# An adaptive-layernorm block with attention and mixture of experts: gates in the last evictions, a three-pass output projection, the second normalisation on ScalarE

## The reference

```python
mod = (silu(c) @ wmod).reshape(B, 6, 1, -1)
sa, ca, ga, sb, cb, gb = (mod[:, i] for i in range(6))
ga = (2 * (ga >= 0) - 1) * maximum(abs(ga), 0.25)       # gb alike
h = layernorm(x) * (1 + ca) + sa
x = x + ga * attention(h, Wq, Wk, Wv, Wo)               # 2 query heads of 128, one key/value head,
                                                        # rotary angles, causal softmax
h = layernorm(x) * (1 + cb) + sb
x = x + gb * experts(h)
# experts: gate = softmax(h @ Wg + bg); thr = sigmoid(h @ Wt + bt) * 0.125
#          w = gate - thr where that is >= 0, else 0; w /= sum(w) (1 for a sum of 0)
#          out = sum over 8 experts e of w[e] * (gelu(h @ W1[e] + b1[e]) @ W2[e] + b2[e]), hidden size 1024
```

## Time and profile before

| what | us |
|---|---|
| median of 3 runs | 1739.81 (1739.69 to 1741.04) |
| the profiled execution | 1741.29 |
| its span, first to last instruction | 1739.5 |
| PE busy | 1723.0 (99%) |
| DVE busy | 1213.2 (70%) |
| POOL busy | 995.8 (57%) |
| ACT busy | 994.9 (57%) |

### The profile page before, as it was taken

One profiled execution on the slowest core, in us unless ns is written; L12 is line 12 of the kernel. 1 busy time (PEld: TensorE's weight loads), 2 busy tenths in 40 slices (PEclk: granted clock), 3 DMA queues, 4 the chain that ended last, 5 costly groups with the idle time before them and its releaser, 6 DMA issues.

```text
span 1739.5 us, 26367 instructions
## 1 busy us (share of the span) xinstructions
PE 1723.0 (99%) x8408; PEld 1448.2 (83%) x8408; DVE 1213.2 (70%) x2275; ACT 994.9 (57%) x1797; POOL 995.8 (57%) x1649
## 2 busy tenths in 40 slices
PE   8999999999999999999999999999999999999998
PEld 7889888898888888888888888888888888888887
DVE  6777778767676666666666678766666666666666
ACT  3766666655665555555555566555555555555553
POOL 5644455336264655647484849374847566574843
PEclk9999999999999999999999999999999999999999
DMA  4000000012111111111112121222301011111202
GB/s 114 26 25 19 26 25 25 11 34 69 23 52 25 50 25 49 37 37 37 37 49 30 47 33 39 61 67 80 110 25 49 25 49 37 37 37 37 37 12 61
DMA packets 92059, 72.54 MB, mean 42 GB/s; under 512 B 11025, under 2 KB 90129, under 8 KB 91921
## 3 DMA queue, kind: packets, MB, share of 16 engines
q1 hardware_dynamic: 91776, 70.79, 15.2%
q10 hardware_dynamic: 144, 0.07, 0.0%
HBM read 62.32 MB, written 8.52 MB: 41 GB/s over the span
## 4 chain that ended last, share of the span: by engine, by line
PE 83%; DVE 2%; issue 1%; ACT 1%; POOL 0%; DVEq 0%; ACTq 0%; POOLq 0%
PE bank L1088 13%; PE bank L1086 13%; PE bank L1087 13%; PE bank L1042 11%; PE bank L1044 11%; PE bank L1043 11%; PE bank L966 2%; PE bank L992 1%; PE bank L1006 1%; PE bank L954 1%; PE bank L955 1%; PE bank L953 1%; PE bank L888 1%; PE bank L878 1%; PE bank L987 1%
## 5 line engine op out<-in xcount | busy, mean ns | idle before, releaser
L1351 ACT ACTIVATE g_sb<-c_sb,b_cols 128x512 f32<-128x512 f32 x384 | 276.3, 720 | 397.0 <-DVE c_sb L1832 293.2
L1679 DVE TENSOR_TENSOR h_lo<-g_sb,h_hi 128x512 fp32r<-128x512 f32 x512 | 390.2, 782 | 101.7 <-ACT h_hi L1355 101.7
L1086 PE MATMUL bank<-h_hi,w_both 128*128 128x512 f32 x1024 | 398.8, 389 | 0.0
L1088 PE MATMUL bank<-h_lo,w_both 128*128 128x512 f32 x1024 | 398.7, 389 | 0.0
L1087 PE MATMUL bank<-h_hi,w_both 128*128 128x512 f32 x1024 | 398.4, 389 | 0.0
L1989 POOL TENSOR_TENSOR h2f<-h2f,y_sb 128x256 f32<-128x256 f32 x216 | 201.0, 963 | 286.0 <-DVE y_sb L1703 286.0
L1042 PE MATMUL bank<-t_hi,w_hi 128*128 128x512 f32 x896 | 352.1, 393 | 4.2 <-DVE p_u L1823 1.6
L1044 PE MATMUL bank<-t_hi,w_lo 128*128 128x512 f32 x896 | 348.9, 389 | 0.0
L1043 PE MATMUL bank<-t_lo,w_hi 128*128 128x512 f32 x896 | 348.8, 389 | 0.0
L1355 ACT ACTIVATE h_hi<-c_sb,b_cols 128x512 fp32r<-128x512 f32 x384 | 271.9, 708 | 0.0
L1088 PEld LDWEIGHTS bank<-h_lo,w_both 128*128 128x128 f32 x1024 | 192.2, 188 | 40.3
(11 more groups left out here) (191 smaller groups left out, 2905.4 us busy)
## 6 DMA issues: line engine op xcount, KB each, us to landing
w_raw<-w_dram SPq DMA_DIRECT2D x128, 256.0 KB, 2.9
g_rows<-gates_scratch SPq DMA_DIRECT2D x32, 512.0 KB, 8.7
x_sb<-x_dram SPq DMA_DIRECT2D x32, 128.0 KB, 2.3
x_scratch<-x_sb SPq DMA_DIRECT2D x32, 128.0 KB, 1.7
x_slabs<-x_scratch SPq DMA_DIRECT2D x4, 512.0 KB, 7.4
out_dram<-x_slabs SPq DMA_DIRECT2D x4, 512.0 KB, 3.1
h2f<-x_scratch SPq DMA_DIRECT2D x4, 512.0 KB, 3.5
wmod_raw<-wmod_dram SPq DMA_DIRECT2D x4, 256.0 KB, 3.7
```

The costliest lines, as they stand in the source:

```text
L1086: nc.tensor.matmul(o, w_hi, h_hi[:, ring, :], start=first, stop=False, skip_group_check=True)
L1088: done_ = nc.tensor.matmul(o, w_hi, h_lo[:, ring, :], start=False, stop=last, skip_group_check=True)
L1351: nc.scalar.activation(g_sb[:, m % 2, :], source, ACT.Gelu_apprx_tanh, bias=bias).then_inc(act_g, 1)
L1679: nc.vector.tensor_tensor(h_lo[:, m % RING, :], g_sb[:, m % 2, :], h_hi[:, m % RING, :].bitcast(F32), ALU.subtract).then_inc(dve_lo, 1)
```

## The change

- **Output projection.** ScalarE's eviction of the attention output now writes a rounded `o_hi`, and VectorE writes `o_lo`, the rest (a new part of stage `O`, semaphore `dve_O`). The gated output weights are split too, once for each batch (`wo`, three steps for one). `project` issues three F32R products for each head, for one fp32 product. The next tile's first `PV` and the projection wait for VectorE's part.
- **Second normalisation.** `xb` goes from VectorE (`(x - mean) * rstd`) to ScalarE (`x * rstd + less_mean`). GpSimd makes `less_mean = -(mean * rstd)` in two more tiny steps at the end of each `rstd`. The input's normalisation waits only for the first four steps.
- **Orders.** Lengths in `parts_of` follow these edits, and all `PATIENCE` numbers are new, so that the order of the attention stage on every engine is another.
- **Gates.** The two gate rows of `pre` are evicted to two tensors in two operations; the attention one lives only for the first stage. `less_max` and `exps` share the memory of `o_out`, and `G1` waits for the old keys' last use.
- **The end.** In group 20, VectorE takes gb of batch 1 as columns (`og_cols`), times b2 (`og_b2`), and a copy of the last expert's weights with tokens on partitions (`g_cols`). The last four evictions apply `og_cols` and `og_b2` and not `g_rows`: three banks on ScalarE, the fourth on VectorE in two halves. After the transposes, one multiply-and-add from PSUM on VectorE (`add_last`: times `g_cols`, plus the piece) takes the place of scaling and addition, and GpSimd has no part in it. The transposes of half 1 are ordered by channel block. The last load of weight rows goes.

```diff
-G1_STEPS, G2_STEPS, WO_STEPS = 2, 12, (4, 1, 4)
+G1_STEPS, G2_STEPS, WO_STEPS = 2, 12, (4, 3, 4)
+RSTD_STEPS = 6
...
     if kind == "rstd":
-        return [("POOL", 1090, [("norm", i, 0, "ACT")])]
+        return [("POOL", 1500, [("norm", i, 0, "ACT")])]
...
     if kind == "xb":
-        return [("DVE", 420, [("rstd", i + BEHIND, 0, "POOL"), ("bT", i - 2, 0, "PE")])]
+        return [("ACT", 480, [("rstd", i + BEHIND, 0, "POOL"), ("bT", i - 2, 0, "PE"), ("Y", i, 0, "DVE")])]
...
-            after += [("O", i - 1, 0, "ACT"), ("qkv", i, 0, "DVE" if TIME[i] >= EARLY else "ACT")]
+            after += [("O", i - 1, 0, "DVE"), ("qkv", i, 0, "DVE" if TIME[i] >= EARLY else "ACT")]
...
-        return [("ACT", 390, [("PV", i, groups_of(i) - 1, "PE"), ("Y", i - 1, 0, "PE")])]
+        return [("ACT", 390, [("PV", i, groups_of(i) - 1, "PE"), ("Y", i - 1, 0, "PE")]),
+                ("DVE", 425, [("O", i, 0, "ACT")])]
     if kind == "Y":
-        return [("PE", 860, [("O", i, 0, "ACT"), ("wo", BATCH[i], 1, "DVE")]),
-                ("DVE", 1300, [("Y", i, 0, "PE"), ("xb", i - 2, 0, "DVE")])]
+        return [("PE", 710, [("O", i, 0, "DVE"), ("wo", BATCH[i], 1, "DVE")]),
+                ("DVE", 1300, [("Y", i, 0, "PE"), ("xb", i - 2, 0, "ACT")])]
...
 PATIENCE = {
-    "PE": {"aT": 452, "bT": 777, "qkv": 886, "rotT": 552, "Y": 651, "pre": 1131, "gate": 1051, "S": 717,
-            "T": 815, "PV": 830},
...
-    "POOL": {"xa": 311, "rope": -1774, "norm": -583, "rstd": -3599, "traw": 2780, "split": -6008},
+    "PE": {"aT": 853, "bT": 900, "qkv": 1076, "rotT": 985, "Y": 940, "pre": 1334, "gate": 1978, "S": 975,
+            "T": 977, "PV": 1001},
...
+    "POOL": {"xa": 1625, "rope": 2132, "norm": 1836, "rstd": 2160, "traw": 352, "split": -1582},
 }
...
                     for h in range(NH):
-                        last = nc.tensor.matmul(bank[:, h * D:(h + 1) * D], o_attn[:, h * P:(h + 1) * P],
-                                                wo_ga[:, BATCH[i], h, :], start=True, stop=True)
+                        to, heads = bank[:, h * D:(h + 1) * D], slice(h * P, (h + 1) * P)
+                        hi, lo = (w[:, BATCH[i], h, :] for w in (wo_hi, wo_lo))
+                        nc.tensor.matmul(to, o_hi[:, heads], hi, start=True, stop=False)
+                        nc.tensor.matmul(to, o_hi[:, heads], lo, start=False, stop=False)
+                        last = nc.tensor.matmul(to, o_lo[:, heads], hi, start=False, stop=True)
...
+                def normalise_x1(i):
+
+                    slot = (i + BEHIND) % 2
+                    act.wait_ge(*done(pool_ln, "rstd", i + BEHIND, 0, RSTD_STEPS))
+                    act.wait_ge(*done(dve_x1, "Y", i))
+                    if i >= 2:
+                        act.wait_ge(*done(pe_bT, "bT", i - 2))
+                    nc.scalar.activation(xb[:, i % 2, :], x1_sb[:, i % 2, :], ACT.Identity, scale=rstd[:, slot, 1:2],
+                                         bias=less_mean[:, slot:slot + 1]).then_inc(act_xb, 1)
...
+                for u, k in ((0, 0), (0, 1), (1, 0)):
...
+                    nc.scalar.activation(y_sb[:, u, k, :], y_banks[u][k], ACT.Identity, scale=og_cols[:, k:k + 1],
+                                         bias=og_b2[:, k:k + 1]).then_inc(act_last, 1)
...
+                            step(nc.vector.tensor_copy(wo_hi[:, i, :, :], both), 2)
+                            step(nc.vector.tensor_tensor(wo_lo[:, i, :, :], both, wo_hi[:, i, :, :].bitcast(F32),
+                                                         ALU.subtract), 3)
...
+                    elif kind == "O":
+
+                        dve.wait_ge(*done(act_O, "O", i))
+                        nc.vector.tensor_tensor(o_lo[:], o_ps[:, 0:NH * P], o_hi[:].bitcast(F32),
+                                                ALU.subtract).then_inc(dve_O, 1)
...
+                def add_last(n, bank):
+
+                    dve.wait_ge(pe_fin, n + 1)
+                    for i in range(2):
+                        t = 2 * n + i
+                        tile = slabs[2 + t // UNIT][:, t % UNIT, :]
+                        last = nc.vector.scalar_tensor_tensor(tile, bank[:, i * D:(i + 1) * D], g_cols[:, t:t + 1], tile,
+                                                              ALU.mult, ALU.add)
+                    last.then_inc(dve_out, 1)
...
-                evict(GROUPS - 1, 1)
-                dve.wait_ge(dve_lo, 4 * GROUPS)
-                for i, (to, bank) in enumerate(((g_sb[:, 0, :], bank_h), (g_sb[:, 1, :], bank_b))):
-                    dve.wait_ge(pe_fin, i + 3)
-                    scaled(to, bank, B - 1, dve_fin)
...
+                add_last(0, bank_a)
+                add_last(1, bank_g)
...
+                for half in (slice(0, UTOK // 2), slice(UTOK // 2, UTOK)):
+                    nc.vector.tensor_scalar(y_sb[:, 1, KD - 1, half], y_banks[1][KD - 1][:, half],
+                                            og_cols[:, KD - 1:KD], og_b2[:, KD - 1:KD], ALU.mult,
+                                            ALU.add).then_inc(dve_last, 1)
+                add_last(2, bank_h)
+                add_last(3, bank_b)
```

163 lines of the change are left out of this document (95 added, 68 removed), and 9 rows, old and new, of the table PATIENCE.

## The result

The changed kernel takes **1736.83 us** (median of 11 runs, 1732.95 to 1739.36), the kernel before 1740.59 on the same chip (11 runs, 1739.69 to 1741.64). The medians are 3.8 us apart, and the ratio is 0.9977 [0.9970, 0.9985], or 4.0 us, where 6.3 were forecast; the time lies in the range, 3.3 us above the forecast. The runs of the new kernel are spread over 6.4 us, those of the old one over 2.0. That is the first sign that something in it differs from run to run.

The account below looks back on a forecast made before the run. The prediction took attention to be bound by the sum of TensorE's turns. From a span of 1739.5 it took 4.8 (projection) and 1.5 (end), all else 0: 1733.2, or 1733.5 for the median; forecast 1731.5 to 1735.5, range 1729.0 to 1738.5.

Parts of the forecast that it names:

- the start gets longer: Rival: GpSimd's extra 2.1 us in the start reach TensorE, giving 1735.6 to 1736.5 us; chance 0.15.
- the gain is waited away: Rival: the projection's 4.8 us pass into TensorE waits for probabilities or low parts, giving 1738.3, no change; chance 0.10.
- Step 1: Output projection, 32 times: six split products take 0.71 us for 0.86, gaining 4.8 us, bounds nothing and 4.8.
- Step 2: Attention output's split: one more VectorE subtraction per tile, about 0.5 us longer hand-over, taken as covered: 0.
- the slower rival: Rival: the output's longer hand-over isn't covered, the next PV waits; 0.5 us per tile costs 16, giving 1749; chance 0.08.
- Step 3: Second normalisation on ScalarE: 32 activations at 0.38 us, 12 us on that engine, 0 on the path.
- Step 4: Two more GpSimd steps per root, 38 roots: 0.70 us each, 27 in all; 0 in the dense part.
- Step 5: Gated output weights: three products for one per batch, and the gates' eviction in two pieces: 0.
- Step 6: The start, first 40 us: input-tile wait and lower clock, 5.2 us in the gap; taken 0, bounds -5.2 and +3.
- Two pulls: In the start: new GpSimd priorities may close the 5.2 us gap; three or so longer roots add 2.1 us.
- Step 7: The end: new evictions and multiply-and-adds bring the last addition from 1736.62 to 1735.15, gain 1.5 us, bounds 0.8 and 2.0.

Follow-up runs that it names:

- e5: The changed kernel with the nine gate columns read 14 times over (126 columns) in each gate product: 1733.82 us, ratio 0.9960 to the kernel before.
- e7: e5 with the output projection as two plain fp32 products of the high parts, same orders and waits, low parts' share left out: 1737.87 us.
- e4: The kernel before with the three-pass output projection alone, its new parts put into the old orders by hand: 1743.55 us, ratio 1.0019.
- e11: e5 with VectorE's subtraction for the output's low part (o_lo) made twice in each tile: 1734.69 us.
- e8: e5 with less_mean written three times, two more tiny GpSimd steps at the end of each root: 1742.17 us.
- e10: e9 with less_mean made by one GpSimd step in place of two in the other 32 roots: 1732.38 us.
- e9: e5 without the two new GpSimd steps in the first six roots, whose less_mean nobody reads: 1731.66 us.
- e3: The kernel before with the new end alone, attention and its orders unchanged: 1739.27 us, ratio 0.9991 [0.9983, 1.0000].
- e6: e5 with the start's two-column conditioning products reading their operand 64 times over (128 columns): 1733.68 us.
- e12: e9 with the start's two-column conditioning products widened to 128 columns as in e6: 1731.37 us, ratio 0.9946 to the kernel before.
- e1: The changed kernel with a 128-column operand (the identity) for the 9-column one in the last five gate stages: 1733.9 us.
- after: The changed kernel itself, with no follow-up edit: 1736.83 us.

## Why the prediction was right, and where it was not

The time fell in the range, but not where the weight lay. It is outside the 1731.5 to 1735.5 that had 0.50, between *the start gets longer* (up to 1736.5) and *the gain is waited away* (1738.3), and what put it there is in neither. The range reached so far for a longer start, so that it held is in part luck. By the prediction's own bound for "faster", 1736.3, the median would even count as no change; 11 runs of each kernel tell 3.8 us from none. The sign that it named, the expert stage starting some 5 us earlier, is missing in the changed kernel (0.8) and there in e5 (6.1).

1. **Step 1, the projection.** The turn is as predicted: 0.71 us at 52.28 for an estimate of 0.71, and 0.15 less than before in like places, as forecast. The gain in time is 4.05 (e7) for 4.8; in the orders of e5, 0.75 us of it are not passed on. The bounds 0 and 4.8 hold for these orders. They don't hold in the old ones: alone, with the same shorter turns, it made the kernel 2.8 us slower (e4), in part by a longer stretch at the lower clock. The prediction let the bound end at nothing, and a part whose new operations stand in no plan can cost more than its whole gain.

2. **Step 2, the hand-over, and the slower rival.** 0 was right for the kernel as changed: 0.421 us per `o_lo`, no wait of TensorE named for it, and doubling it costs 0.87 (e11). The argument was only half right. It rested on slack seen in the kernel before and on the length planned in; e11 shows the cover only for the new order. In the old one the rival's mechanism was at work at one place at least: at 140.55 TensorE waits 1.8 us for `pT_lo`, queued behind `o_lo` and the splitting of the weights.

3. **Step 3, the normalisation on ScalarE.** The size was wrong, 0.599 us for 0.38, the row of a copy from PSUM. It cost no time in the kernel as changed, since ScalarE had the room (265 of 384 us). e8 shows how near it was to costing: there `xb` is what TensorE waits for, 2.8 us in four places.

4. **Step 4, two more GpSimd steps.** The sentence that failed as a reason is "In the dense part GpSimd is at half load: 0". For the change itself e10 supports the 0 there. But half load was no proof of slack: 0.73 more in each root, at the same half load, costs 8.35 us (e8), some 5 of it after 40 us. The share of busy time says nothing of how soon each result is wanted.

5. **Step 5, the gated weights.** No run prices it by itself. In the new orders, where the second batch's splitting is planned in, TensorE's waits show nothing of it; e4 shows it unplanned.

6. **Step 6, the start.** Two pulls were named, and both exist. TensorE's wait for an input tile from GpSimd went from 2.5 us to 0.2, and the one for VectorE's from 1.4 to 1.7:

```profile
PE bank L905 <- DVE xa L1667: 1.7, 2, 1.1
...
PE bank L905 <- POOL xa L2003: 0.2, 1, 0.2
```

The other pull is the new steps. Here they are, in a timeline of POOL in e5, ahead of the rotation that feeds TensorE:

```profile
21.27 0.19 POOL L1969 TENSOR_TENSOR scaled_mean<-mv,rstd 128x1 f32<-128x1 f32 x1
21.62 0.23 POOL L1972 TENSOR_SCALAR less_mean<-scaled_mean 128x1 f32<-128x1 f32 x1 [0.16 <-POOL scaled_mean L1969]
21.81 1.11 POOL L1988 TENSOR_TENSOR rot_c<-qk,cos_sb 128x384 f32<-128x384 f32 x1
```

21.81 - 21.27 = 0.54 us for the two, where 0.70 was estimated, and again at 27.66 and 29.37; taking out those that nobody reads gave 2.2 (e9) for the 2.1 of the prediction. That the two agree is chance: the 2.1 was three roots of 0.70, and e9 relieves six, all ahead of 40 us. The balance in the forecast was 0. e5 is 6.45 below the kernel before, of which 4.05 are the projection and 1.47 the end, and 0.9 is left over; but the interval of e3 alone reaches from 0 to 3 us, so a gain in the start is not shown. What failed for the new kernel is the price of the clock. Half of TensorE's busy time in the slow stretch, 2.7 us, was put down as recoverable; e6 recovered 0.14, and e12, with GpSimd out of the way, 0.29, neither of them clear of the scatter. TensorE's time at half clock replaced waiting, and the 0.2 us above would be 1.3 (for this tile and a rotation) with the shorter stretch of e5. For the kernel before it may have been right. There the stretch, from 30.4 to 37.2, outlasts the wait that ends at 31.79 and nothing is waited for behind it, as in the slowest run of e6. No run took it out there.

7. **Step 7, the end.** 1.5 forecast, 1.47 measured (e3). The pieces differ and cancel: ScalarE's eviction takes 0.78 for 0.69, VectorE's halves 1.00 for the pair and not 0.75, the multiply-and-adds 1.66 for four and not 1.75. The transposes start at 1731.89, before the last halves are ready, which the estimate had not used.

**What was missing.** 4.8 + 1.5 was the forecast's gain; 4.05 + 1.47 and the 0.9 left over are 6.4, what the change has in it (e5 against before), so the forecast of 1733.5 is near the time of e5, 1733.82. The changed kernel gives 3.0 of it back in its median, and 5.1 in the profiled execution, to TensorE's lower clock after gate stages that the new order puts at other places, and to what comes with it (in the profiled execution the wait of 0.7). The prediction read the clock row only in the start and looked at the new priorities only for GpSimd. That `gate` went from 1051 to 1978 for TensorE, against 853 to 1076 for all others but `pre`, stood in the diff. None of the rivals had the mechanism: "gain waited away" gave nearly the measured time (1738.3), but by waits spread over attention, and TensorE has only the 0.7 us at one place. e1 and e5 tell the two apart, since neither changes what an engine must wait for.

The Trainium skill (TensorE: Matmul & The Clock Gate, What's actually happening) says that the gate follows how busy TensorE has been. By the busy column of the profile this case doesn't bear that out: 3.50 of 3.50 us ahead of the fall at 401.5, and 6.80 of 6.80 within it. The same page says that how many products run slowly differs from run to run in one kernel; the traces agree for the start, where the same program has a stretch of 6.8 us in the profile of after and of 3.4 in that of e5.

**What stays open.** Why the stretches come in some executions and are shorter or elsewhere in others; where exactly e4 loses its 7.6 us against the expectation; what takes e10's 0.3 us back at 360 to 380 us. An order with the old places of the gates and everything else new was not tried, and neither was the second normalisation's move by itself.

## What to carry to other kernels

When an order of work is made anew, read the granted clock around TensorE's narrowest products in several executions: a TensorE that is busy all the time can be at half speed, and a spread that grows between runs is the cheapest sign of it. Where such a product's turn is hardly set by its columns, reading its operand several times over kept the clock up here: it cost some 0.7 us and left 3.0 of 1737 gained. An engine at half load is not an engine with slack: test it by repeating one of its small steps, and take unread work out of the start before speeding anything up there.

## What was not expected of the hardware

- Products of 9 and of 126 columns (fp32, 128x128 weights) follow each other at nearly the same distance, 0.106 and 0.111 us, and only the narrow ones were followed by a granted clock of 0.50 late in attention.
- The 10.2 us at the lower clock late in attention cost some 4.6 of TensorE's time. A stretch of 3.4 in the start, ahead of waits of TensorE, cost too little to measure (0.14); one of the same length just behind its last wait cost 1.65, half its length.
- ScalarE's scale-and-bias by partition from SBUF takes 0.599 us for 128x256, against 0.383 for its copy of that size from PSUM.
- Two chained GpSimd operations on one element per partition take 0.53 to 0.72 us from the start of the first to the next operation, though their rows say 0.19 and 0.23.
